# Group 0 of a hypergraph block: c2 by one product with ones, half of W2 scaled by ScalarE, squares ahead of the readings

## The chip, the core and the metric

The kernel runs on one core of one Trainium2 chip. The metric is the device time of one execution in microseconds (us). The engines are TensorE (PE; its weight loads are PEld), VectorE (DVE), ScalarE (ACT), GpSimd (POOL) and SyncE (SP), which only issues transfers here. Each runs its own list of instructions in the order written; semaphores tie the lists together.

## What is computed

For each of 64 graphs (128 nodes, 256 features) a hypergraph convolution to 512 features, ReLU, a layer norm with gamma and beta, a second convolution back to 256 features, two additions of x, and a last layer norm:

```
H = (adj != 0);  w = adj[:, 0, :]
conv(x, W, b) = Dn * H @ (Be * H^T @ (x @ W^T)) + b      Dn = 1 / (H @ w),  Be = 1 / H.sum(axis=1)
h = relu(conv(x, W1, b1))
h = layer_norm(h) * gamma + beta
out = layer_norm(x + conv(h, W2, b2) + x)
```

The norm over the 512 hidden features is folded into the second weight. W2 is turned, scaled by gamma and centred. What beta contributes, the vector c2 = W2 @ beta (256 numbers), is the same for all nodes and is added when the second layer's product is read.

## The kernel before

The 64 graphs are worked on in G = 16 groups of four. For one group the steps are: h = (adj != 0) on VectorE (make_h, L665); its transpose, for the first three groups on TensorE (turn_h, L245), then by DMA (L182); its reading with row counts by ScalarE (read_ht, L487); inverse counts (make_b, L688) and scaling (make_htb, L501); the product s (make_s, L255), degrees (make_d, L674), the scaled matrix a (L510), its transpose (L266, L518); u = x times that (make_u, L272); four products v with W1 (make_v, L285), each followed by a relu (L544) on ScalarE; the four r chunks are split into a high part on GpSimd (L985) and a low part on VectorE (L726); the products with W2 (make_g, L307), one for each graph; the second norm's statistics; y (make_y, L333); z; the last norm; the store.

The variance of a node comes from the squares of r: ScalarE squares the four chunks (square, L551), VectorE adds them in two pairs and then the pairs (add_squares, L744: three additions, the last gives q_sb), TensorE turns q into bank 3 of bank_g (turn_q, L325), and ScalarE sums it (sum_q, L565). make_g(i, 3) writes the same bank 3 afterwards, and waits for those sums.

Products in high and low parts are written as three terms. Plain fp32 products take two records each in the trace.

W2 is made ready during the first layer of group 0. TensorE turns it into banks 2 and 3 of bank_g, VectorE scales the four chunks by gamma into w2_g (scale_w2, L781) and adds them (L867, L870); one product with ones gives the sums over all hidden features (sum_w2, L387), VectorE centres by them (centre_w2, L789); ScalarE rounds to w2_hi (L615), VectorE takes the rest, w2_lo (split_w2, L796). make_g(0, 0) waits for w2_lo.

For c2, ScalarE copies the turned W2 into w2_t (L610), GpSimd writes beta along 128 columns (L1021), and TensorE makes four products, two before make_s(1) and two after (make_c2, L392); VectorE copies the result (read_c2, L801) ahead of make_h(3).

The order is written out by hand for each engine. On TensorE group 0 is lines L415 to L468, on ScalarE L604 to L661, on VectorE L861 to L925. A number in brackets after a step is the group, and after it the chunk or graph: make_v(0, 2) is chunk 2 of group 0.

Of the kernel before, what the change touches and what calls it, by code (L numbers as in the profile page):

```python
# [20 lines left out]
def hypergraph_block(nc, x, adj, W1, b1, gamma, beta, W2, b2, out):  # L21
# [13 lines left out]
    with ExitStack() as ctx:  # L35
        def sb(name, shape, dt=F32):
            return ctx.enter_context(nc.sbuf_tensor(name, shape, dt))

        def sem(name):
            return ctx.enter_context(nc.semaphore(name))  # L40
# [11 lines left out]
        vec = sb("vec", [P, 3 * KH])  # L52
        w1_hi = sb("w1_hi", [P, KD, HID], F32R)
        w1_lo = sb("w1_lo", [P, KD, HID], F32R)
        w2_t = sb("w2_t", [P, KH, DOUT])
        w2_g = sb("w2_g", [P, KH, DOUT])
        w2_sum = sb("w2_sum", [P, KH // 2, DOUT])
        beta_b = sb("beta_b", [P, KH, P])
        w2_hi = sb("w2_hi", [P, KH, W2COLS], F32R)
        w2_lo = sb("w2_lo", [P, KH, DOUT], F32R)  # L60
        c2 = sb("c2", [P, DOUT])
# [66 lines left out]
        consts_zeroed, consts_ready = sem("consts_zeroed"), sem("consts_ready")  # L128
        vec_turned, vec_ready = sem("vec_turned"), sem("vec_ready")
        w1_turned, w1_hi_ready, w1_ready = sem("w1_turned"), sem("w1_hi_ready"), sem("w1_ready")  # L130
        w2_turned, w2_t_ready, w2_scaled = sem("w2_turned"), sem("w2_t_ready"), sem("w2_scaled")
        w2_added, w2_summed, w2_centred = sem("w2_added"), sem("w2_summed"), sem("w2_centred")
        w2_hi_ready, w2_ready = sem("w2_hi_ready"), sem("w2_ready")
        beta_ready, c2_made, c2_ready = sem("beta_ready"), sem("c2_made"), sem("c2_ready")
        h_ready, h_turned, ht_ready = sem("h_ready"), sem("h_turned"), sem("ht_ready")
        h_dma_turned = sem("h_dma_turned")
        d_stored, d_row_in = sem("d_stored"), [sem("d_row_even"), sem("d_row_odd")]
# [106 lines left out]
        def _(pe):  # L244
            def turn_h(j):  # L245
                pe.wait_ge(h_ready, j + 1)
                if j == 1:
                    pe.wait_ge(at_ready, 1)
                elif j == 2:
                    pe.wait_ge(a_ready, 2)  # L250
                for n in range(PER):
                    mm = pe.transpose(bank_h_bf[:, graph(n)], h_sb[:, j % 2, n], ident_b[:, :])
                mm.then_inc(h_turned, 1)
# [18 lines left out]
            def make_u(j):  # L272
                pe.wait_ge(at_ready, j + 1)
                pe.wait_ge(x_in[j % 3], landed(j, 3))
                for c in range(KD):
                    if j == 1:
                        pe.wait_ge(relu_ready, 3 + c)
                    else:
                        pe.wait_ge(z_ready, 2 * j - 3 + c)
                    for n in range(PER):  # L280
                        mm = pe.matmul(bank_v[:, c, graph(n)], x_sb[:, j % 3, n, graph(c)], at_sb[:, j % 3, n],  # L281
                                       start=True, stop=True)
                    mm.then_inc(u_made, 1)
# [41 lines left out]
            def turn_q(i):  # L325
                pe.wait_ge(q_ready, i + 1)
                pe.wait_ge(q_summed, i * 2)
                pe.wait_ge(g_ready, i * 2)
                for n in range(PER):
                    mm = pe.transpose(turned_q[:, graph(n)], q_sb[:, graph(n)], ident[:, :])  # L330
                mm.then_inc(q_turned, 1)
# [57 lines left out]
                pe.matmul(bank_g[:, 0, 0:DOUT], ones[:, :], w2_sum[:, 0], start=True,  # L389
                          stop=True).then_inc(w2_summed, 1)  # L390

            def make_c2(chunks):  # L392
                pe.wait_ge(beta_ready, 1)
                pe.wait_ge(w2_t_ready, 1)
                for k in chunks:
                    mm = pe.matmul(bank_g[:, 1, 0:DOUT], beta_b[:, k], w2_t[:, k], start=(k == 0), stop=(k == KH - 1))
                if chunks[-1] == KH - 1:
                    mm.then_inc(c2_made, 1)

            pe.wait_ge(consts_ready, 2)  # L400
            for _ in range(WARM_UP):
# [21 lines left out]
            make_v(0, 2)  # L423
            sum_w2()
            make_v(0, 3)
            make_c2([0, 1])
            make_s(1)
            make_c2([2, 3])

            pe.wait_ge(w2_ready, 1)  # L430
            for i in range(G):
                make_g(i, 0)
                if i == 0:
                    turn_a(1)
                    turn_h(2)
                    pe.wait_ge(c2_ready, 1)
                make_g(i, 1)
                if i == 0:
                    make_u(1)
                if i == LAST:  # L440
                    turn_q(i)
                elif i:
                    make_v(i + 1, 0)
                make_g(i, 2)
                if i == 0:
                    turn_q(0)
                    make_v(1, 0)
                    make_s(2)
                elif i < LAST:
                    make_v(i + 1, 1)  # L450
                make_g(i, 3)
                if i == LAST:
                    break
                if i == 0:
                    make_v(1, 1)
                make_v(i + 1, 2)
                make_v(i + 1, 3)
                if i == 0:
# [27 lines left out]
        def _(act):  # L486
# [23 lines left out]
            def make_a(j):  # L510
                act.wait_ge(d_ready, j + 1)
                act.wait_ge(a_turned, j)
                for n in range(PER):
                    ins = nc.scalar.activation(a_sb[:, n], s_parts[:, n // 2, n % 2, 0:P], ACT.Copy,
                                               scale=dinv[:, j % 2, n:n + 1])
                ins.then_inc(a_ready, 1)

            def read_at(j):  # L518
                act.wait_ge(a_turned, j + 1)
                nc.scalar.activation(at_sb[:, j % 3].rearrange("p n c -> p (n c)"), turned_a,  # L520
                                     ACT.Copy).then_inc(at_ready, 1)
# [22 lines left out]
            def relu(i, k):  # L544
                act.wait_ge(v_made, i * KH + (k + 1))
                if i:
                    act.wait_ge(r_lo_ready, (i - 1) * KH + (k + 1))
                nc.scalar.activation(r_sb[:, k], bank_v[:, k % 2], ACT.Relu,  # L548
                                     bias=vec[:, k:k + 1]).then_inc(relu_ready, 1)
# [45 lines left out]
            for n in each(0):  # L595
# [7 lines left out]
            split_w1(1)  # L603
            split_u(0)  # L604
            act.wait_ge(vec_ready, 1)
            relu(0, 0)
            read_ht(1)
            relu(0, 1)
            act.wait_ge(w2_scaled, 2)
            nc.scalar.activation(w2_t[:, :, :].rearrange("p k o -> p (k o)"),  # L610
                                 bank_g[:, 2:4].rearrange("p b o -> p (b o)"), ACT.Copy).then_inc(w2_t_ready, 1)
            relu(0, 2)
            make_htb(1)
            act.wait_ge(w2_centred, 1)
            nc.scalar.activation(w2_hi[:, :, 0:DOUT], w2_g[:, :, :], ACT.Copy).then_inc(w2_hi_ready, 1)  # L615
            relu(0, 3)
            make_a(1)
            read_at(1)
            read_ht(2)
            square(0, 0)  # L620
            square(0, 1)
            square(0, 2)
            square(0, 3)

            for i in range(G):
                if i == 0:
# [37 lines left out]
        def _(dve):  # L664
# [113 lines left out]
                nc.vector.tensor_scalar(var2[:, last, part], mv_sb[:, last, part, 1], EPS, None,  # L778
                                        ALU.add).then_inc(var2_ready, 1)

            def scale_w2(chunks):  # L781
                dve.wait_ge(w2_turned, 1 + chunks[0] // (KH // 2))
                dve.wait_ge(vec_ready, 1)
                for k in chunks:
                    ins = nc.vector.tensor_scalar(w2_g[:, k], bank_g[:, 2 + k // 2, (k % 2) * DOUT:(k % 2 + 1) * DOUT],
                                                  vec[:, KH + k:KH + k + 1], None, ALU.mult)
                ins.then_inc(w2_scaled, 1)
# [8 lines left out]
            def split_w2():  # L796
                dve.wait_ge(w2_hi_ready, 1)
                nc.vector.tensor_tensor(w2_lo[:, :, :], w2_g[:, :, :], w2_hi[:, :, 0:DOUT].bitcast(F32),  # L798
                                        ALU.subtract).then_inc(w2_ready, 1)

            def read_c2():  # L801
                dve.wait_ge(c2_made, 1)
                nc.vector.tensor_copy(c2[:, :], bank_g[:, 1, 0:DOUT]).then_inc(c2_ready, 1)

            def make_first_h(half):
                dve.wait_ge(adj_in[0] if half else first_adj, 16)
# [54 lines left out]
            make_h(1)  # L861
            split_w1(1)
            split_u(0)
            scale_w2(range(KH // 2))
            scale_w2(range(KH // 2, KH))
            dve.wait_ge(w2_scaled, 2)
            nc.vector.tensor_tensor(w2_sum[:, :, :], w2_g[:, 0:2], w2_g[:, 2:4], ALU.add).then_inc(w2_added, 1)  # L867
            make_b(1)
            dve.wait_ge(w2_added, 1)
# [1 line left out]
            split_r(0, 0)  # L871
            centre_w2()
            split_r(0, 1)
            make_h(2)
            split_w2()
            make_d(1)
            split_r(0, 2)
            split_r(0, 3)
            read_c2()
            make_h(3)  # L880
            make_b(2)

            for i in range(LAST):
                if i == 0:
# [69 lines left out]
        def _(pool):  # L954
# [63 lines left out]
            copy_w(1)  # L1018
            pool.wait_ge(consts_ready, 3)
            pool.wait_ge(vec_ready, 1)  # L1020
            for k in range(KH):  # L1021
                ins = nc.gpsimd.tensor_scalar(beta_b[:, k], ones[:, :], vec[:, 2 * KH + k:2 * KH + k + 1], 1.0,
                                              ALU.mult, ALU.mult)
            ins.then_inc(beta_ready, 1)
            pool.wait_ge(weights_in[3], 16)
            nc.gpsimd.tensor_scalar(b2_half[:, :], b2_half[:, :], 0.5, 1.0, ALU.mult,
                                    ALU.mult).then_inc(consts_ready, 1)
# [47 lines left out]
```

## Time and profile before

| what | value |
|---|---|
| median of 3 runs | 287.64 us (287.48 to 287.89) |
| the profiled execution, its time | 287.23 us |
| its span, first to last instruction | 285.4 us |
| share of TensorE in the chain that ended last | 91% |
| TensorE busy | 276.9 us (97%) |
| VectorE busy | 229.5 us (80%) |
| ScalarE busy | 196.2 us (69%) |
| GpSimd busy | 134.9 us (47%) |
| mean granted clock of TensorE | 0.995 |

How to read it: the engines overlap, so the busy times don't add up to the span. A view in order of time gives for each instruction (or merged run of like ones) its start, its length, the line of the kernel, what it writes and from what, and in brackets how long the engine had stood idle before it and which instruction released it. Matmuls are pipelined, so a record lasts longer than the step to the next one: where a cost on TensorE is meant, take the difference of two starts. On VectorE and ScalarE too the next instruction can start up to some 0.1 us before the one before it ends.

### The profile page before, as it was taken

The page shows a single profiled execution, that of the slowest core. Times are in us where ns is not written, and L with a number is a line of the kernel's source. Part 1 is how long each engine was busy: PE and PEld are TensorE (multiplying, and loading weights), DVE is VectorE, ACT ScalarE, POOL GpSimd, SP SyncE. Part 2 cuts the span into 40 slices and gives each one's busy share as a digit, 9 for nine tenths or more (in the row PEclk, how much of TensorE's full clock was granted, in tenths as well). Part 3 has the DMA queues.
Part 4 walks back from the last instruction along what each step waited for, and adds up shares of the span by engine and source line. Part 5 has one row for each costly group of instructions (what it writes and reads, how often), then busy time and mean ns, then how long its engine had stood idle before and what let it go on. Part 6 is the DMA issues. An engine that isn't in the chain of part 4 may idle for free.

```text
span 285.4 us, 5786 instructions
## 1 busy us (share of the span) xinstructions
PE 276.9 (97%) x1820; PEld 247.8 (87%) x1820; DVE 229.5 (80%) x646; ACT 196.2 (69%) x560; POOL 134.9 (47%) x194
## 2 busy tenths in 40 slices
PE   7999999999999999999999999999999999999991
PEld 6889899898988989898998989899898989889890
DVE  3795688887889878887978878797987879696784
ACT  3588967877767678766767776676678775573714
POOL 2341546436372744536363553636364364526362
PEclk9999999999999999999999999999999999999998
DMA  6912042344324134433433333522423332020014
GB/s 217 332 52 69 3 129 39 92 126 116 114 63 158 57 97 128 111 113 92 147 54 119 112 92 112 111 94 55 149 39 92 94 93 76 37 73 3 21 54 147
DMA packets 37270, 27.70 MB, mean 97 GB/s; under 512 B 10028, under 2 KB 35320, under 8 KB 37240
## 3 DMA queue, kind: packets, MB, share of 16 engines
q1 hardware_dynamic: 37136, 27.30, 33.8%
q8 instruction: 14, 0.23, 0.3%
q14 instruction: 16, 0.13, 0.2%
q10 hardware_dynamic: 104, 0.04, 0.1%
HBM read 17.21 MB, written 8.42 MB: 90 GB/s over the span
## 4 chain that ended last, share of the span: by engine, by line
PE 91%; ACT 3%; DVE 3%; issue 1%; POOL 1%; DVEq 0%; POOLq 0%; ACTq 0%
PE bank_v L303 30%; PE bank_g L320 10%; PE bank_v L337 10%; PE bank_g L313 10%; PE bank_g L315 10%; PE bank_v L281 8%; PE bank_s L262 4%; PE bank_g L330 3%; PE bank_s L402 1%; ACT ht_sb L497 1%; ACT sq_sb L555 1%; PE bank_g L383 1%; DVE bn_sb L933 1%; DVE q_sb L742 0%; DVE pair_sb L735 0%
## 5 line engine op out<-in xcount | busy, mean ns | idle before, releaser
L981 POOL TENSOR_TENSOR xb_sb<-x_sb,b_half 128x512 f32<-128x512 f32 (+1 forms) x31 | 41.1, 1329 | 76.0 <-DVE r_lo L730 51.1
L548 ACT ACTIVATE r_sb<-bank_v,vec 128x512 f32<-128x512 f32 x64 | 44.2, 690 | 38.0 <-PE bank_v L303 37.4
L313 PE MATMUL bank_g<-w_hi,r_hi 128*128 128x258 f32 x256 | 65.6, 288 | 0.0
L315 PE MATMUL bank_g<-w_lo,r_hi 128*128 128x256 f32 x256 | 63.8, 282 | 0.0
L989 POOL TENSOR_SCALAR r_hi<-r_sb 128x512 fp32r<-128x512 f32 x64 | 43.6, 682 | 39.8 <-ACT r_sb L548 39.8
L303 PE MATMUL bank_v<-u_hi,w_lo 128*128 128x512 f32 x128 | 50.8, 397 | 0.0
L303 PE MATMUL bank_v<-u_lo,w_hi 128*128 128x512 f32 x128 | 50.8, 397 | 0.0
L303 PE MATMUL bank_v<-u_hi,w_hi 128*128 128x512 f32 x128 | 50.7, 396 | 0.0
L313 PEld LDWEIGHTS bank_g<-w_hi,r_hi 128*128 128x128 f32 x256 | 48.3, 189 | 1.7 <-DVE w_lo L798 0.3
L730 DVE TENSOR_TENSOR r_lo<-r_sb,r_hi 128x512 fp32r<-128x512 f32 x64 | 48.9, 785 | 0.9 <-POOL r_hi L989 0.9
L315 PEld LDWEIGHTS bank_g<-w_lo,r_hi 128*128 128x128 f32 x256 | 48.1, 188 | 1.2
L320 PE MATMUL bank_g<-w_hi,r_lo 128*128 128x258 f32 x256 | 41.5, 283 | 0.1
L555 ACT ACTIVATE sq_sb<-r_sb 128x512 f32<-128x512 f32 x64 | 40.2, 634 | 1.9
L721 DVE SCALAR_TENSOR_TENSOR g_sb<-bank_g,rstd,c 128x256 f32<-128x256 f32 x64 | 28.1, 480 | 12.8 <-POOL rstd L965 12.8
L320 PEld LDWEIGHTS bank_g<-w_hi,r_lo 128*128 128x128 f32 x256 | 35.3, 189 | 0.3 <-DVE r_lo L730 0.3
L560 ACT ACTIVATE z_sb<-z_sb,shift,rstd 128x256 f32<-128x256 f32 x60 | 32.3, 586 | 4.5 <-POOL shift L1004 4.5
L526 ACT ACTIVATE u_hi<-bank_v 128x512 fp32r<-128x512 f32 x30 | 17.9, 600 | 24.3 <-PE bank_v L281 24.3
L337 PE MATMUL bank_v<-g_sb,at_sb 128*128 128x256 f32 x120 | 31.7, 387 | 0.1
L965 POOL TENSOR_TENSOR rstd<-stat,half_power 128x2 f32<-128x2 f32 x32 | 22.6, 708 | 18.3 <-DVE stat L711 18.1
L281 PE MATMUL bank_v<-at_sb,x_sb 128*128 128x128 f32 x240 | 29.4, 276 | 0.0
L303 PEld LDWEIGHTS bank_v<-u_lo,w_hi 128*128 128x128 f32 x128 | 24.0, 188 | 6.1 <-DVE u_lo L698 0.7
L337 PEld LDWEIGHTS bank_v<-g_sb,at_sb 128*128 128x128 f32 x120 | 21.5, 189 | 8.2 <-issue 5.3
(119 smaller groups left out, 457.6 us busy)
## 6 DMA issues: line engine op xcount, KB each, us to landing
x_sb<-in_x_dram SPq DMA_DIRECT2D x16, 512.0 KB, 3.9
out_dram<-z_sb SPq DMA_DIRECT2D x15, 512.0 KB, 3.2
adj_sb<-in_adj_dram SPq DMA_DIRECT2D x15, 256.0 KB, 3.7
d_row<-d_rows SPq DMA_DIRECT2D x13, 256.0 KB, 3.7
w_raw<-in_L_gnn_W_dram SPq DMA_DIRECT2D x2, 512.0 KB, 4.9
out_dram<-z_sb SPq DMA_DIRECT2D x2, 256.0 KB, 2.4
adj_sb<-in_adj_dram SPq DMA_DIRECT2D x2, 128.0 KB, 2.4
turned_h<-h_sb SPq DMA_TRANSPOSE x13, 2.4
```

Of the source, the lines that this page charges most:

```text
L281: mm = pe.matmul(bank_v[:, c, graph(n)], x_sb[:, j % 3, n, graph(c)], at_sb[:, j % 3, n], start=True, stop=True)
L303: mm = pe.matmul(bank_v[:, k % 2], w[:, c, graph(k)], u[:, c], start=(m == 0), stop=(m == len(terms) - 1))
L313: pe.matmul(bank_g[:, n, 0:W2COLS], r_hi[:, i % 2, k, graph(n)], w2_hi[:, k], start=(k == 0), stop=False)
L315: pe.matmul(bank_g[:, n, 0:DOUT], r_hi[:, i % 2, k, graph(n)], w2_lo[:, k], start=False, stop=False, skip_group_check=True)
L320: mm = pe.matmul(bank_g[:, n, 0:W2COLS], r_lo[:, i % 2, k, graph(n)], w2_hi[:, k], start=False, stop=(k == KH - 1))
L337: mm = pe.matmul(bank_v[:, half, (n % 2) * DOUT:(n % 2 + 1) * DOUT], at_sb[:, i % 3, n], g_sb[:, n], start=True, stop=True)
L548: nc.scalar.activation(r_sb[:, k], bank_v[:, k % 2], ACT.Relu, bias=vec[:, k:k + 1]).then_inc(relu_ready, 1)
L555: nc.scalar.activation(sq_sb[:, k], r_sb[:, k], ACT.Square).then_inc(sq_ready, 1)
L560: ins = nc.scalar.activation(z_sb[:, i % 2, n], z_sb[:, i % 2, n], ACT.Identity, bias=shift2[:, n:n + 1], scale=rstd2[:, 0, n:n + 1])
L730: nc.vector.tensor_tensor(r_lo[:, i % 2, k], r_sb[:, k], r_hi[:, i % 2, k].bitcast(F32), ALU.subtract).then_inc(r_lo_ready, 1)
L981: nc.gpsimd.tensor_tensor(xb_sb[:, i % 2, part], x_sb[:, i % 3, part], b2_half[:, :].unsqueeze(1).to_broadcast([P, n, DOUT]), ALU.add).the ...
L989: nc.gpsimd.tensor_scalar(r_hi[:, i % 2, k], r_sb[:, k], 1.0, 1.0, ALU.mult, ALU.mult).then_inc(r_hi_ready, 1)
```

## The change

The four c2 products are replaced by one. VectorE forms, in four instructions, the sum over the chunks of turned W2 times beta, straight from banks 2 and 3, and TensorE multiplies it once by ones, into bank 3. This product stands behind make_u(1) and ahead of make_g(0, 2); turn_q(0), which writes the same bank, waits for the copy of c2. The copies w2_t and beta_b are gone. ScalarE scales chunks 0 and 1 of W2 by gamma ahead of relu(0, 0), and VectorE only chunks 2 and 3. turn_h(2) goes behind make_g(0, 1); make_h(2) behind the last r_lo of group 0; read_c2 behind make_b(2). ScalarE squares chunk 0 ahead of make_a(1), chunk 1 ahead of read_at(1), and reads ht(2) last.

```diff
 TensorE
-            def make_c2(chunks):
-                pe.wait_ge(beta_ready, 1)
-                pe.wait_ge(w2_t_ready, 1)
-                for k in chunks:
-                    mm = pe.matmul(bank_g[:, 1, 0:DOUT], beta_b[:, k], w2_t[:, k], start=(k == 0), stop=(k == KH - 1))
...
+            def make_c2():
+                pe.wait_ge(beta_added, KH)
+                pe.matmul(bank_g[:, 3, 0:DOUT], ones[:, :], w2_beta[:, (KH - 1) % 2], start=True,
+                          stop=True).then_inc(c2_made, 1)
...
             make_v(0, 3)
-            make_c2([0, 1])
             make_s(1)
-            make_c2([2, 3])
...
                 if i == 0:
                     turn_a(1)
-                    turn_h(2)
-                    pe.wait_ge(c2_ready, 1)
                 make_g(i, 1)
                 if i == 0:
+                    turn_h(2)
                     make_u(1)
+                    make_c2()
...
                 make_g(i, 2)
                 if i == 0:
+                    pe.wait_ge(c2_ready, 1)
                     turn_q(0)
 ScalarE
             act.wait_ge(vec_ready, 1)
+            act.wait_ge(w2_turned, 1)
+            for k in range(KH // 2):
+                ins = nc.scalar.activation(w2_g[:, k], bank_g[:, 2, k * DOUT:(k + 1) * DOUT], ACT.Copy,
+                                           scale=vec[:, KH + k:KH + k + 1])
+            ins.then_inc(w2_low_scaled, 1)
             relu(0, 0)
...
-            act.wait_ge(w2_scaled, 2)
-            nc.scalar.activation(w2_t[:, :, :].rearrange("p k o -> p (k o)"),
-                                 bank_g[:, 2:4].rearrange("p b o -> p (b o)"), ACT.Copy).then_inc(w2_t_ready, 1)
...
             relu(0, 3)
+            square(0, 0)
             make_a(1)
+            square(0, 1)
             read_at(1)
-            read_ht(2)
-            square(0, 0)
-            square(0, 1)
             square(0, 2)
             square(0, 3)
+            read_ht(2)
 VectorE
+            def add_beta(k):
+                w2_t, scale = bank_g[:, 2 + k // 2, (k % 2) * DOUT:(k % 2 + 1) * DOUT], vec[:, 2 * KH + k:2 * KH + k + 1]
+                if k == 0:
+                    ins = nc.vector.tensor_scalar(w2_beta[:, 0], w2_t, scale, None, ALU.mult)
+                else:
+                    dve.wait_ge(beta_added, k)
+                    ins = nc.vector.scalar_tensor_tensor(out=w2_beta[:, k % 2], in0=w2_t, scalar=scale,
+                                                         in1=w2_beta[:, (k - 1) % 2], op0=ALU.mult, op1=ALU.add)
+                ins.then_inc(beta_added, 1)
...
             split_r(0, 1)
-            make_h(2)
             split_w2()
             make_d(1)
             split_r(0, 2)
             split_r(0, 3)
-            read_c2()
+            make_h(2)
+            for k in range(KH):
+                add_beta(k)
             make_h(3)
             make_b(2)
+            read_c2()
 
             for i in range(LAST):
                 if i == 0:
                     add_squares(0)
 GpSimd
-            for k in range(KH):
-                ins = nc.gpsimd.tensor_scalar(beta_b[:, k], ones[:, :], vec[:, 2 * KH + k:2 * KH + k + 1], 1.0,
-                                              ALU.mult, ALU.mult)
-            ins.then_inc(beta_ready, 1)
```

## Rows read from the trace of the kernel before

**Rows 1.** Waits of TensorE: engine, line, releaser: us in total, times, longest.

```profile
PE bank_s L402 <- POOL ident L1011: 1.8, 1, 1.8
PE bank_g L330 <- DVE q_sb L742: 0.3, 1, 0.3
```

**Rows 2.** Timeline of TensorE: start, us, line, what [idle before <- releaser].

```profile
16.54 0.59 PE L389 MATMUL bank_g<-w_sum,ones 128*128 128x256 f32 x2
...
18.37 1.03 PE L396 MATMUL bank_g<-w_t,beta_b 128*128 128x256 f32 x4
19.24 1.05 PE L262 MATMUL bank_s<-htb_sb,ht_sb 128*128 128x129 f32 x8
20.13 1.03 PE L396 MATMUL bank_g<-w_t,beta_b 128*128 128x256 f32 x4
21.06 0.39 PE L313 MATMUL bank_g<-w_hi,r_hi 128*128 128x258 f32 x1
...
25.12 1.95 PE L281 MATMUL bank_v<-at_sb,x_sb 128*128 128x128 f32 x16
26.82 0.37 PE L313 MATMUL bank_g<-w_hi,r_hi 128*128 128x258 f32 x1
...
28.82 0.66 PE L330 MATMUL bank_g<-ident,q_sb 128*128 128x128 f32 x4 [0.32 <-DVE q_sb L742]
29.42 0.50 PE L303 MATMUL bank_v<-u_hi,w_hi 128*128 128x512 f32 x1
```

**Rows 3.** Timeline of the weight loads, the first of make_g(0, 0).

```profile
21.06 0.19 PEld L313 LDWEIGHTS bank_g<-w_hi,r_hi 128*128 128x128 f32 x1 [0.31 <-DVE w_lo L798]
```

**Rows 4.** Timeline of VectorE.

```profile
17.25 1.40 DVE L792 SCALAR_TENSOR_TENSOR w_g<-bank_g,w_g 128x256 f32<-128x256 f32 x4
...
19.78 1.23 DVE L798 TENSOR_TENSOR w_lo<-w_g,w_hi 128x1024 fp32r<-128x1024 f32 x1 [0.19 <-ACT w_hi L615]
...
21.41 1.28 DVE L730 TENSOR_TENSOR r_lo<-r_sb,r_hi 128x512 fp32r<-128x512 f32 x2
22.61 0.42 DVE L803 COPY c<-bank_g 128x256 f32<-128x256 f32 x1
22.94 0.42 DVE L671 TENSOR_SCALAR h_sb<-adj_sb 128x512 bf16<-128x512 f32 x1
...
26.31 0.69 DVE L735 TENSOR_TENSOR pair_sb<-sq_sb 128x512 f32<-128x512 f32 x1 [0.65 <-ACT sq_sb L555]
27.35 0.69 DVE L735 TENSOR_TENSOR pair_sb<-sq_sb 128x512 f32<-128x512 f32 x1 [0.35 <-ACT sq_sb L555]
28.07 0.69 DVE L742 TENSOR_TENSOR q_sb<-pair_sb 128x512 f32<-128x512 f32 x1
28.68 1.28 DVE L698 TENSOR_TENSOR u_lo<-bank_v,u_hi 128x512 fp32r<-128x512 f32 x2
```

**Rows 5.** Timeline of ScalarE.

```profile
13.71 0.69 ACT L548 ACTIVATE r_sb<-bank_v,vec 128x512 f32<-128x512 f32 x1 [1.38 <-PE bank_v L303]
...
18.69 1.06 ACT L615 ACTIVATE w_hi<-w_g 128x1024 fp32r<-128x1024 f32 x1
...
24.10 0.27 ACT L497 ACTIVATE ht_sb<-bank_s 128x128 f32<-128x128 bf16 x1
...
25.10 2.21 ACT L555 ACTIVATE sq_sb<-r_sb 128x512 f32<-128x512 f32 x4
...
30.48 0.28 ACT L570 ACTIVATE scratch<-bank_g 128x128 f32<-128x128 f32 x1
```

**Rows 6.** Groups of VectorE by form, the reading of g: busy us, mean ns.

```profile
L721 DVE SCALAR_TENSOR_TENSOR g_sb<-bank_g,rstd,c 128x256 f32<-128x256 f32 x64 | 28.1, 480 | 12.8 <-POOL rstd L965 12.8
```

**Rows 7.** The page, part 6: the DMA transposes of h, us from issue to landing.

```profile
turned_h<-h_sb SPq DMA_TRANSPOSE x13, 2.4
```

**Rows 8.** Stretches of 1 us in the tail: busy of PE, PEld, DVE, ACT, POOL, granted clock.

```profile
281.00:282.00 1.00, 0.00 (x0) 0.00 (x0) 0.36 (x1) 0.64 (x2) 0.54 (x1) 1.00 0.57 205
...
283.00:284.00 1.00, 0.00 (x0) 0.00 (x0) 0.00 (x0) 0.00 (x0) 0.00 (x0) 0.50 1.00 343
```

More of the change, by code:

```diff
@@ L54, in hypergraph_block @@
         w1_lo = sb("w1_lo", [P, KD, HID], F32R)
-        w2_t = sb("w2_t", [P, KH, DOUT])
+        w2_beta = sb("w2_beta", [P, 2, DOUT])
         w2_g = sb("w2_g", [P, KH, DOUT])
         w2_sum = sb("w2_sum", [P, KH // 2, DOUT])
-        beta_b = sb("beta_b", [P, KH, P])
         w2_hi = sb("w2_hi", [P, KH, W2COLS], F32R)
@@ L130, in hypergraph_block @@
         w1_turned, w1_hi_ready, w1_ready = sem("w1_turned"), sem("w1_hi_ready"), sem("w1_ready")
-        w2_turned, w2_t_ready, w2_scaled = sem("w2_turned"), sem("w2_t_ready"), sem("w2_scaled")
+        w2_turned, w2_low_scaled, w2_scaled = sem("w2_turned"), sem("w2_low_scaled"), sem("w2_scaled")
         w2_added, w2_summed, w2_centred = sem("w2_added"), sem("w2_summed"), sem("w2_centred")
         w2_hi_ready, w2_ready = sem("w2_hi_ready"), sem("w2_ready")
-        beta_ready, c2_made, c2_ready = sem("beta_ready"), sem("c2_made"), sem("c2_ready")
+        beta_added, c2_made, c2_ready = sem("beta_added"), sem("c2_made"), sem("c2_ready")
         h_ready, h_turned, ht_ready = sem("h_ready"), sem("h_turned"), sem("ht_ready")
@@ L390, in sum_w2 @@
                           stop=True).then_inc(w2_summed, 1)
-            def make_c2(chunks):
-                pe.wait_ge(beta_ready, 1)
-                pe.wait_ge(w2_t_ready, 1)
-                for k in chunks:
-                    mm = pe.matmul(bank_g[:, 1, 0:DOUT], beta_b[:, k], w2_t[:, k], start=(k == 0), stop=(k == KH - 1))
-                if chunks[-1] == KH - 1:
-                    mm.then_inc(c2_made, 1)
+            def make_c2():
+                pe.wait_ge(beta_added, KH)
+                pe.matmul(bank_g[:, 3, 0:DOUT], ones[:, :], w2_beta[:, (KH - 1) % 2], start=True,
+                          stop=True).then_inc(c2_made, 1)
             pe.wait_ge(consts_ready, 2)
@@ L779, in make_var2, with scale_w2 @@
                                         ALU.add).then_inc(var2_ready, 1)
-            def scale_w2(chunks):
-                dve.wait_ge(w2_turned, 1 + chunks[0] // (KH // 2))
+            def scale_w2():
+                dve.wait_ge(w2_turned, 2)
                 dve.wait_ge(vec_ready, 1)
-                for k in chunks:
+                for k in range(KH // 2, KH):
                     ins = nc.vector.tensor_scalar(w2_g[:, k], bank_g[:, 2 + k // 2, (k % 2) * DOUT:(k % 2 + 1) * DOUT],
@@ L799, in split_w2 @@
                                         ALU.subtract).then_inc(w2_ready, 1)
+            def add_beta(k):
[7 more added lines that the diff above has]
+                ins.then_inc(beta_added, 1)
             def read_c2():
                 dve.wait_ge(c2_made, 1)
-                nc.vector.tensor_copy(c2[:, :], bank_g[:, 1, 0:DOUT]).then_inc(c2_ready, 1)
+                nc.vector.tensor_copy(c2[:, :], bank_g[:, 3, 0:DOUT]).then_inc(c2_ready, 1)
             def make_first_h(half):
@@ L863, in _ @@
             split_u(0)
-            scale_w2(range(KH // 2))
-            scale_w2(range(KH // 2, KH))
-            dve.wait_ge(w2_scaled, 2)
+            scale_w2()
+            dve.wait_ge(w2_scaled, 1)
+            dve.wait_ge(w2_low_scaled, 1)
             nc.vector.tensor_tensor(w2_sum[:, :, :], w2_g[:, 0:2], w2_g[:, 2:4], ALU.add).then_inc(w2_added, 1)
```

## The prediction, made before the changed kernel was run

> **What bounds the kernel now.** I read the waits of TensorE first: over the whole run its matmul stream stopped for another engine twice, 1.8 us at the very start and 0.3 us before the turning of q [rows 1]. So every us by which TensorE's stream is stretched or halted is a us on the end, and nothing later can absorb it, because no later idle of TensorE exists to shrink. (The page's chain of work says the same: nearly all of it lies on TensorE.) All that the change touches lies in group 0, between 12 and 30 us. There I read the start times on TensorE [rows 2], its weight loads, which show what the next product was held by [rows 3], and the two engines that feed it [rows 4, 5].
>
> What the reader is to see in these: make_g(0, 0) starts at 21.06, and its weight load had waited 0.31 us for w2_lo, which ends at 19.78 + 1.23 = 21.01 [rows 3, 4]. The second half of the c2 products, at 20.13, occupies TensorE only up to that moment [rows 2]: it fills a wait. The next stop is q: VectorE finishes q_sb at 28.07 + 0.69 = 28.76, the transposes start at 28.82, 0.06 later [rows 2, 4]. The one after is the low half of u: u_lo's first chunk ends at 28.68 + 0.69 = 29.37 and make_v(1, 0) starts at 29.42 [rows 2, 4]. From there TensorE runs without a stop [rows 1].
>
> **The change, part by part.** The sum is made for the start of turn_q(0) and of make_v(1, 0), 28.82 and 29.42 before; what they shift by, the end shifts by.
>
> (a) Eight c2 records leave TensorE ahead of make_g(0, 0): 0.87 us at 18.37 to 19.24 and some 0.87 us from 20.13 [rows 2]. They gain nothing by themselves, because w2_lo decides the start. make_s(1) can follow, though not before htb(1), which is ready when ScalarE goes to w2_hi, at 18.69 [rows 5]; it takes 0.89 us (19.24 to 20.13), so TensorE then stands idle from about 19.55 to 21.0, 1.4 us.
>
> (b) How much sooner w2_lo can be. ScalarE loses the copy w2_t, as long as w2_hi's pass over the same 1024 columns, 1.06 us [rows 5]. But w2_hi, at 18.69, also needs VectorE's centring, 17.25 + 1.40 = 18.65, and that needs the sum product, two records from 16.54 to 17.13, which can start no sooner since it stands behind make_v(0, 2) [rows 2, 4]. So of the whole copy at most 0.1 us arrives at w2_lo. I take 0.05 us (bounds 0 and 0.1).
>
> (c) Scaling half of W2 on ScalarE: two instructions of 256 columns. The trace has none of that form; a pass over 1024 columns takes 1.06 us, one relu over 512 takes 0.69, so each lies between a quarter of the first and the whole of the second: 0.5 to 1.4 us for both. They fall into a wait of 1.38 us ahead of relu(0, 0) at 13.71 [rows 5]. Cost nothing. VectorE is freed of two scalings, but what it made with them, the sum of W2, is wanted by a product that stands behind make_v(0, 2) on TensorE and was on hand when it got there: no wait of TensorE lies there [rows 1]. Gain nothing. The four beta broadcasts taken from GpSimd ran ahead of its first splitting of r: nothing either way.
>
> (d) After w2_lo VectorE keeps its order, d(1) and the last two r_lo (21.41 + 1.28 = 22.69), which make_g(0, 0) needs for its last product [rows 4]. So make_u(1) starts at 25.12 - 0.05 = 25.07: turn_h(2) merely changes places with make_g(0, 1) (0.20 us either side), and the transposes of a are as before.
>
> (e) VectorE's new sum. It starts after make_h(2), about 22.9. Four instructions of 128x256 from PSUM with a scalar by partition: the nearest row is the reading of g, 0.48 us [rows 6], and each waits for the one before, so 4 x 0.51 = 2.0 us, done by 24.9; make_h(3), 0.42, by 25.3. The bound below is the centring, 1.40 us for four with no waits [rows 4]; above I allow 0.6 us each, 2.4 us. TensorE asks for the sum at 26.77: cover of 1 us or more by either bound. Cost nothing. make_h(2) comes 3.3 us later and make_h(3) 1.9 us later; on SP's queue the load of adj(5) waits for the one, the DMA transpose of h(3) for the other, and the load of adj(6) behind it. The transposes take 2.4 us from issue to landing in the median [rows 7]; from 25.3 that is 27.7, and ScalarE comes to read ht(3) only near 28.8. Adj(5) isn't read before group 1. Nothing; the price of a transpose 2 us longer than that would be 1 us on ScalarE ahead of sum_q(0), which (g) shows to have a us to spare.
>
> (f) The new c2 product: one fp32 product of 256 columns with ones, two records. Four such take 0.87 us [rows 2], so 0.44 us. It stands behind make_u(1), at 26.82 - 0.05 = 26.77. The result is complete 0.59 us after its start (as the sum product's), at 27.36, and VectorE sees it 0.05 us later: 27.41.
>
> (g) The step that decides. read_c2 stands on VectorE ahead of add_squares(0). In the kernel before it ran at 22.61, when c2 was long there, and add_squares could start at 26.31 as soon as ScalarE had two squares; the last square ended at 25.10 + 2.21 = 27.31 [rows 4, 5]. Now ScalarE squares before the reading of at(1) and ht(2) and ends near 25.3, 2 us sooner, but VectorE cannot use it: it has finished make_b(2) at about 26.8 (turn_h(2) ends at 25.1, ScalarE's four readings, 1.0 us from 24.10 to 25.10 [rows 5], and two small instructions follow) and waits for c2 until 27.41. What is queued behind that wait is the chain for q. The copy of c2 costs 0.42 us, of which 0.33 before the next starts (22.61 to 22.94): 27.74. First pair 0.61, second pair 0.69 + 0.03, q 0.69, in all 2.02 us (by the two r_lo of 1.28 us, and from 27.35 to 28.07) [rows 4]: q at 29.76. turn_q(0) at 29.82 instead of 28.82: **1.00 us later**. split_u(1) follows q on VectorE as before, so make_v(1, 0) starts 1.00 us later too. make_g(0, 2) ends, with the 0.44 us of c2 in front of it, at about 28.7, so TensorE idles 1.1 us there instead of 0.3. ScalarE's sum_q(0) came at 30.48 only since ScalarE was busy till then [rows 5]; with q turned at 30.5 it hardly moves, and make_g(0, 3), at 32.7, doesn't wait for it.
>
> Sum: -0.05 (w2_lo) + 1.05 (q) = +1.00 us, carried to the end. The profiled execution has a span of 285.4 us and took 287.23; the median of the runs is 287.64, 0.4 above. On the profiled execution I expect a span of 286.4 and a time of 288.2; on the median, 288.6 us. For the likeliest case alone the unknown terms are the sooner w2_lo (0 to 0.1), the c2 product with its latency (0.5 to 0.8) and the copy (0.33 to 0.5), so +0.8 to +1.3 and 288.4 to 288.9.
>
> **The clock.** TensorE's granted clock is 1.00 (2.4 GHz) in every stretch up to the tail; at the end TensorE does nothing after 279.3, and the clock is still 1.00 in 281 to 282 and is 0.50 in 283 to 284 [rows 8]. So it outlasted over 2.7 us without work; the two new idle stretches, 1.4 and 1.1 us with 8 us of products between, are shorter. I count no loss. The Trainium skill, page "TensorE: Matmul & The Clock Gate", Part 1, says that an engine which has been idle is set back to 1.2 GHz and must be busy for a time to get 2.4 GHz back; by it the idle that this change opens could cost a slow stretch, and that speaks against the change. As a mechanism here: if one of the stops brought the clock to 0.50, as it stands after 283 [rows 8], a slow stretch as long as the one seen there (some 2.8 us to the end of the span) would do half its work, 1.4 us more.
>
> **Rivals.**
> Squares sooner makes q sooner (the other side). If VectorE were not held, the adds could run from 26.8 and q would not hold TensorE: turn_q(0) directly behind make_g(0, 2), which now ends near 28.7, and make_v(1, 0) at 29.15 to 29.3, 0.1 to 0.3 sooner: 287.4. For it: the squares really are 2 us sooner, and the wait for them was the last to end. It decides if c2 is on hand when VectorE gets to read_c2, so if make_u(1) ended by 26.2, 0.6 us earlier than it can by (d). Little speaks for it: 0.10.
> Part of the loss comes back, so that +0.2 to +0.55 is left: the copy of c2 and the pair adds cost less than I took, or TensorE had hidden slack in group 1. Against it, TensorE starts its products there at their steady spacing: 0.10; about 288.0.
> The chain ahead of w2_lo shrinks by the whole copy (1.06 us) and c2 is hidden: 286.6. Against it stands the centring, as in (b): 0.04.
> The clock falls in one of the stops: 1.00 + 1.4 = 2.4 us, 290.0: 0.05.
> The forecast has 0.71.
>
> **How the numbers follow.** About 0.2% (0.58 us) is what a measurement of this kernel can tell from no change. Slower by more than that: forecast and clock, 0.76. Within it: the first two rivals, 0.20. Faster: 0.04. The range, 287.6 to 289.1, takes in the forecast's own bounds with 0.2 us of spread between runs and the partly returned loss; it leaves out most of the quicker cases and the clock, about 2 in 10.
>
> **What would show it.** In the trace of the changed kernel: an idle stretch of TensorE of 1.4 us ending at 21.0, with w2_lo as its releaser; c2's product at 26.8; VectorE idle before the copy of c2 with that product as releaser; the copy at 27.4, the first pair add right behind it though the squares had been done since about 25.3; TensorE idle for 1.1 us before the transposes of q, now at 29.8; then start times of group 1 one us later than before to the end. I am wrong if c2's product comes well ahead of 26, if VectorE doesn't wait at the copy, if the granted clock drops below 1.00 near 20 or 30 us, or if TensorE closes the gap later on.

## The result, and the profile after

The changed kernel took 288.39 us (median of 11 runs, 288.13 to 288.82) against 287.48 us (287.17 to 287.89, 11 runs) for the kernel before beside it: ratio 1.0033, 95% interval 1.0024 to 1.0043. The profiled execution took 288.13 us, with a span of 286.3 us, 0.9 more than before. The forecast was 1.0 us slower.

TensorE's waits after (engine, line, releaser: us in total, times, longest), to be read beside [rows 1]:

```profile
PE bank_s L398 <- POOL ident L1021: 1.8, 1, 1.8
PE bank_g L312 <- DVE w_lo L795: 1.2, 1, 1.2
PE bank_g L329 <- issue: 1.1, 1, 1.1
```

The 0.3 us ahead of the transposes of q has become 1.1 us, and 1.2 us of idle has opened ahead of make_g(0, 0). "issue" in the third line says that no releaser was recognised; the VectorE rows below show which one it was. The fourth line of that view, 0.6 us for L365, lies in the first 6 us and has no part in this.

TensorE in order of time after (start, us, line, what, idle before), beside [rows 2]:

```profile
18.64 1.16 PE L261 MATMUL bank_s<-htb_sb,ht_sb 128*128 128x129 f32 x8
20.98 0.39 PE L312 MATMUL bank_g<-w_hi,r_hi 128*128 128x258 f32 x1 [1.19 <-DVE w_lo L795]
...
25.00 2.00 PE L280 MATMUL bank_v<-at_sb,x_sb 128*128 128x128 f32 x16
26.84 0.60 PE L393 MATMUL bank_g<-w_beta,ones 128*128 128x256 f32 x2
27.09 0.47 PE L312 MATMUL bank_g<-w_hi,r_hi 128*128 128x258 f32 x1
...
29.93 0.63 PE L329 MATMUL bank_g<-ident,q_sb 128*128 128x128 f32 x4 [1.06 <-issue]
30.48 0.50 PE L302 MATMUL bank_v<-u_hi,w_hi 128*128 128x512 f32 x1
```

VectorE after, beside [rows 4]:

```profile
19.70 1.23 DVE L795 TENSOR_TENSOR w_lo<-w_g,w_hi 128x1024 fp32r<-128x1024 f32 x1 [0.53 <-ACT w_hi L612]
...
22.53 0.42 DVE L668 TENSOR_SCALAR h_sb<-adj_sb 128x512 bf16<-128x512 f32 x1
22.86 0.47 DVE L802 TENSOR_SCALAR w_beta<-bank_g,vec 128x256 f32<-128x256 f32 x1
23.37 1.52 DVE L805 SCALAR_TENSOR_TENSOR w_beta<-bank_g,vec,w_beta 128x256 f32<-128x256 f32 x3
24.81 0.42 DVE L668 TENSOR_SCALAR h_sb<-adj_sb 128x512 bf16<-128x512 f32 x1
26.38 0.17 DVE L687 TENSOR_SCALAR binv<-members 128x4 f32<-128x4 f32 x1 [1.15 <-ACT ht_sb L492]
26.58 0.18 DVE L690 RECIPROCAL binv<-binv 128x4 f32<-128x4 f32 x1
27.48 0.42 DVE L811 COPY c<-bank_g 128x256 f32<-128x256 f32 x1 [0.72 <-PE bank_g L393]
27.82 1.28 DVE L732 TENSOR_TENSOR pair_sb<-sq_sb 128x512 f32<-128x512 f32 x2
29.14 0.69 DVE L739 TENSOR_TENSOR q_sb<-pair_sb 128x512 f32<-128x512 f32 x1
```

ScalarE after, beside [rows 5]:

```profile
12.22 0.83 ACT L603 ACTIVATE w_g<-bank_g,vec 128x256 f32<-128x256 f32 x2
13.64 0.69 ACT L543 ACTIVATE r_sb<-bank_v,vec 128x512 f32<-128x512 f32 x1 [0.59 <-PE bank_v L302]
...
18.61 1.06 ACT L612 ACTIVATE w_hi<-w_g 128x1024 fp32r<-128x1024 f32 x1
...
24.02 1.14 ACT L550 ACTIVATE sq_sb<-r_sb 128x512 f32<-128x512 f32 x2
...
30.60 0.28 ACT L565 ACTIVATE scratch<-bank_g 128x128 f32<-128x128 f32 x1 [0.62 <-PE bank_g L329]
```

Read them together. The squares end at 24.02 + 1.14 = 25.16. VectorE does nothing from 25.2 to 26.38, then two small instructions, then nothing for 0.72 us until c2 is made (26.84 + 0.60 = 27.44). Only behind the copy, at 27.82, does it begin to add squares that have lain ready for 2.7 us. It finishes q at 29.83; the transposes start at 29.93.

**A measure that is steadier than the span.** The start of make_g(0, 0) differed between the profiled executions of this study, 20.98 to 21.79. It follows what comes before it: the first transposes of W1 began at 6.69 in the executions before and after and at 7.16 in e7 below. What put them off I didn't follow up. All that the change and the experiments touch behind w2_lo lies between the start of make_g(0, 0) and the start of make_v(1, 0). From the second turning of q on, all ten profiled executions took the same time to the start of the last product on the banks of s: 235.71 to 235.76 us. So I cut each timeline at three starts (all in us):

| kernel | make_g(0, 0) | to turn_q(0) | to make_v(1, 0) | from there to turn_q(1) | ratio to before, 95% interval |
|---|---|---|---|---|---|
| before | 21.06 | 7.76 | 8.36 | 12.95 | |
| changed | 20.98 | 8.95 | 9.50 | 12.87 | 1.0033 (1.0024 to 1.0043) |
| e1, c2 ahead of u | 21.58 | 8.13 | 8.68 | 12.87 | 1.0014 (1.0005 to 1.0022) |
| e2, copy behind the pairs | 21.38 | 8.00 | 8.55 | 12.87 | 1.0000 (0.9991 to 1.0009) |
| e3, squares late | 21.54 | 8.99 | 9.54 | 12.94 | 1.0048 (1.0035 to 1.0060) |
| e4, squares only, in before | 21.38 | 7.60 | 8.20 | 12.86 | 0.9995 (0.9986 to 1.0004) |
| e5, changed again | 21.05 | 8.94 | 9.50 | 12.86 | 1.0045 (1.0029 to 1.0061) |
| e6, c2 late in before | 21.22 | 9.36 | 9.92 | 12.86 | 1.0061 (1.0040 to 1.0082) |
| e7, squares and adds | 21.79 | 7.31 | 7.66 | 13.08 | 0.9983 (0.9974 to 0.9992) |
| e8, c2 in the gap | 21.08 | 7.31 | 7.66 | 13.06 | 0.9984 (0.9972 to 0.9996) |

For the changed kernel: 9.50 - 8.36 = +1.14, start -0.08, group 1 -0.08, and the rest of the stream -0.05; the last product starts at 279.06 against 278.13, +0.93, which is the 0.9 us of the span and of the medians.

### The profile page after: what moved, and what is told of

Read it like the earlier page. It is cut to its first block, busy times and chain, and to the rows that moved or that the text cites. A ratio compares the mean times of both kernels' runs of the same rounds, so it can differ in the third digit from the quotient of the medians.

```text
span 286.3 us, 5772 instructions
## 1 busy us (share of the span) xinstructions
PE 275.2 (96%) x1814; PEld 246.1 (86%) x1814; DVE 229.8 (80%) x648; ACT 196.8 (69%) x561; POOL 134.0 (47%) x190
## 4 chain that ended last, share of the span: by engine, by line
PE 93%; DVE 3%; issue 1%; ACT 1%; POOL 1%; DVEq 0%; POOLq 0%
PE bank_v L302 31%; PE bank_g L319 11%; PE bank_g L312 11%; PE bank_g L314 10%; PE bank_v L336 10%; PE bank_v L280 9%; PE bank_s L261 4%; PE bank_g L329 3%; PE bank_s L398 1%; PE bank_g L382 1%; DVE bn_sb L943 1%; DVE w_g L789 0%; DVE w_lo L795 0%; PE bank_s L365 0%; ACT w_hi L612 0%
## 5 line engine op out<-in xcount | busy, mean ns | idle before, releaser
L999 POOL TENSOR_SCALAR r_hi<-r_sb 128x512 fp32r<-128x512 f32 x64 | 44.3, 692 | 38.8 <-ACT r_sb L543 38.8
```

What stands on the lines that cost most here:

```text
L999: nc.gpsimd.tensor_scalar(r_hi[:, i % 2, k], r_sb[:, k], 1.0, 1.0, ALU.mult, ALU.mult).then_inc(r_hi_ready, 1)
```

## The experiments

The theory: VectorE's copy of c2 stands ahead of the adds of the squares, c2 is made only behind make_u(1), and so q and with it TensorE wait. The rival: the cost is TensorE's own, the c2 product where nothing hides it. A second rival: it depends on how soon the squares come.

**e1, c2 sooner on TensorE.**

```diff
-                    make_u(1)
-                    make_c2()
+                    make_c2()
+                    make_u(1)
```

> The changed kernel with one move on TensorE: the c2 product ahead of make_u(1) instead of behind it. Same work on every engine. Theory (VectorE's wait for c2, ahead of the adds of the squares, holds q): c2 is made by 25.6, VectorE copies it right behind make_b(2) with no wait, at 26.7, the adds start at 27.0 and not 27.8, turn_q(0) starts at 29.1 and not 29.93, make_v(1, 0) at 29.7 and not 30.48: 0.8 us faster than the changed kernel, about 0.1% slower than the kernel before. Rival (the 0.44 us of the c2 product in TensorE's stream behind the hidden place, plus the idle ahead of make_g(0, 0), is the cost): nothing changes, 0.3% slower than the kernel before.

Measured: 287.79 us, 1.0014 (1.0005 to 1.0022). From make_g(0, 0) to make_v(1, 0) 8.68 us, 0.82 less than in the changed kernel, where 0.8 was expected. VectorE in e1:

```profile
27.19 0.18 DVE L690 RECIPROCAL binv<-binv 128x4 f32<-128x4 f32 x1
27.29 0.39 DVE L811 COPY c<-bank_g 128x256 f32<-128x256 f32 x1
27.60 1.28 DVE L732 TENSOR_TENSOR pair_sb<-sq_sb 128x512 f32<-128x512 f32 x2
```

The copy follows make_b(2) with no wait, and the adds 0.31 us later. TensorE's work is the same to the product, only its order differs. The first rival falls; by it nothing would have changed.

**e2, the copy behind the pair adds.**

```diff
             make_b(2)
-            read_c2()
...
                 if i == 0:
-                    add_squares(0)
+                    add_pair(0, 0)
+                    add_pair(0, 1)
+                    read_c2()
+                    add_pairs(0)
```

> The changed kernel with one move on VectorE: the copy of c2 between the two pair adds and the last add of group 0, instead of ahead of all three. TensorE's order is untouched. Theory: the pair adds start at 26.7, the copy follows at 27.9 without a wait, q is done at 28.9, turn_q(0) starts at 29.0, make_v(1, 0) at 29.6: 0.9 us faster than the changed kernel, 0 to 0.1% slower than the kernel before. Rival (cost lies in TensorE's stream): no change against the changed kernel, 0.3% slower than the kernel before.

Measured: 287.29 us, 1.0000 (0.9991 to 1.0009): the loss is gone. 8.55 us to make_v(1, 0), 0.95 less than in the changed kernel. VectorE in e2:

```profile
27.08 1.26 DVE L732 TENSOR_TENSOR pair_sb<-sq_sb 128x512 f32<-128x512 f32 x2
28.26 0.42 DVE L811 COPY c<-bank_g 128x256 f32<-128x256 f32 x1
28.59 0.68 DVE L739 TENSOR_TENSOR q_sb<-pair_sb 128x512 f32<-128x512 f32 x1
```

and TensorE, the end of make_g(0, 2) and the transposes of q:

```profile
28.64 0.64 PE L319 MATMUL bank_g<-w_hi,r_lo 128*128 128x258 f32 x4
29.38 0.63 PE L329 MATMUL bank_g<-ident,q_sb 128*128 128x128 f32 x4
```

The c2 product stands where it stood, in TensorE's stream behind make_u(1), and the copy is as long as before. Only what was queued behind the wait has changed. It was not the product, nor the copy's length, but the wait ahead of the adds.

Differences of starts show how much of the loss is TensorE's own. From the start of make_g(0, 0) to the last four products of make_g(0, 2) it takes 7.26 us here and 7.25 in the changed kernel, against 6.80 before: the product costs 0.45 us of its stream. From those four products to the transposes of q it takes 0.49 us in e7 and e8 below, where q is early, 0.96 in the kernel before, 1.70 in the changed kernel and 0.74 here. So TensorE waited 0.47 us for q before the change, which is room for the product, and waits 1.21 us after it. In e2 it still waits 0.25 us, although no idle is listed, because a matmul record is longer than the step to the next one; q, done at 29.27, is what sets the remaining 0.19 us against the kernel before.

**e3, the squares in their old order, in the changed kernel.**

```diff
             relu(0, 3)
-            square(0, 0)
             make_a(1)
-            square(0, 1)
             read_at(1)
+            read_ht(2)
+            square(0, 0)
+            square(0, 1)
             square(0, 2)
             square(0, 3)
-            read_ht(2)
```

> The changed kernel with ScalarE's old order: the four squares of group 0 behind the readings of at(1) and ht(2). Theory: the squares end at 28.3 instead of 25.2, but VectorE gets to its adds only at 27.8 and needs the last two squares at 28.4, so q and turn_q(0) move by 0 to 0.1 us; sum_q(0) ends near 32.8, just as make_g(0, 3) asks for it: the same as the changed kernel within 0.2 us. Rival (how soon the squares are there decides q): q follows the last square by 1.4 us plus some queueing and comes 1 to 3 us later, 0.4 to 1% slower than the changed kernel.

Measured: 288.84 us, 1.0048 (1.0035 to 1.0060). The squares end at 26.77 + 2.20 = 28.97, 7.4 us after make_g(0, 0) starts, against 4.2 us in the changed kernel, and make_v(1, 0) comes 9.54 us after it instead of 9.50. VectorE in e3:

```profile
28.03 0.42 DVE L811 COPY c<-bank_g 128x256 f32<-128x256 f32 x1 [0.72 <-PE bank_g L393]
28.37 1.33 DVE L732 TENSOR_TENSOR pair_sb<-sq_sb 128x512 f32<-128x512 f32 x2
29.73 0.69 DVE L739 TENSOR_TENSOR q_sb<-pair_sb 128x512 f32<-128x512 f32 x1
```

Three us on the squares moved q by 0.04 us. Behind the wait for c2 the new order is worth almost nothing. The trace bears out "the same within 0.2 us" (0.04, and 0.07 in group 1); the ratio, with an interval that overlaps those of both measurements of the changed kernel, can't tell a tenth.

**e4, the squares' order alone, in the kernel before.** The edit is the reverse of e3's, made to the kernel before.

> The kernel before with the one part 'squares of group 0 sooner': ScalarE squares chunk 0 ahead of make_a(1), chunk 1 ahead of read_at(1), chunks 2 and 3 ahead of read_ht(2). Nothing else. Theory (VectorE's list in order decides q): make_b(2), ahead of the adds, now waits for the later reading of ht(2), to 26.7; the adds end at 28.7 against 28.76, turn_q(0) starts at most 0.1 us sooner: the same as the kernel before within 0.1%. Rival (the squares were the bound and their coming sooner by 2 us frees q): turn_q(0) directly behind make_g(0, 2), make_v(1, 0) 0.3 to 0.5 us sooner, 0.1 to 0.2% faster.

Measured: 287.10 us, 0.9995 (0.9986 to 1.0004): the same. By the trace turn_q(0) comes 0.16 us sooner (7.60 for 7.76), a little more than the 0.1 expected and far from the 2 us by which the squares came sooner. VectorE in e4:

```profile
23.26 0.42 DVE L671 TENSOR_SCALAR h_sb<-adj_sb 128x512 bf16<-128x512 f32 x1
26.63 0.17 DVE L690 TENSOR_SCALAR binv<-members 128x4 f32<-128x4 f32 x1 [2.95 <-ACT ht_sb L497]
26.84 0.18 DVE L693 RECIPROCAL binv<-binv 128x4 f32<-128x4 f32 x1
26.93 1.26 DVE L735 TENSOR_TENSOR pair_sb<-sq_sb 128x512 f32<-128x512 f32 x2
```

Here c2 is early and no wait for it exists, and still VectorE stands for 2.95 us with squares at hand, because make_b(2) is next in its list and waits for ht(2), whose reading the new order has put behind the squares. What ScalarE gives sooner, VectorE's order takes back for the most part. The second rival falls in both kernels.

**e5, the changed kernel again**, beside e6 to e8.

> The changed kernel itself, beside the three that follow: 0.3% slower than the kernel before. From the start of make_g(0, 0) to the start of make_v(1, 0) 9.5 us, against 8.36 in the kernel before.

Measured: 288.67 us, 1.0045 (1.0029 to 1.0061), and 9.50 us to make_v(1, 0) once more. The ratio is a tenth of a per cent above the first one, with an interval that overlaps its; the trace gives the same times to 0.01 us.

**e6, the cause alone, in the kernel before.** The products go into bank 3, the last two behind make_u(1), and the copy ahead of the adds.

```diff
             make_s(1)
-            make_c2([2, 3])
...
                     make_u(1)
+                    make_c2([2, 3])
...
+                    pe.wait_ge(c2_ready, 1)
                     turn_q(0)
...
             split_r(0, 3)
-            read_c2()
             make_h(3)
             make_b(2)
+            read_c2()
```

> The kernel before with the suspected cause alone: its four c2 products (into bank 3), the last two of them moved behind make_u(1), and the copy of c2 moved behind make_b(2), ahead of the adds of the squares; turn_q(0) waits for the copy. ScalarE's order, the copy w2_t and the scaling of W2 stay as they were. Theory (c2 late, and its copy ahead of the adds): the two products take 0.87 us behind make_u(1), c2 is complete about 7.0 us after make_g(0, 0) starts, VectorE waits for it with the squares at hand or nearly so, q follows 2.4 us later, and make_g(0, 0) to make_v(1, 0) takes 9.8 to 9.9 us instead of 8.36: 0.45 to 0.5% slower than the kernel before. Rival (the loss comes from the other parts, squares and scaling): only TensorE's own 0.87 us less the wait of 0.3 us it had there, 0.2% slower.

Measured: 288.82 us, 1.0061 (1.0040 to 1.0082); 9.92 us to make_v(1, 0), where 9.8 to 9.9 was expected. TensorE in e6, the two late products:

```profile
27.06 1.03 PE L396 MATMUL bank_g<-w_t,beta_b 128*128 128x256 f32 x4
```

and VectorE behind them:

```profile
28.13 0.42 DVE L803 COPY c<-bank_g 128x256 f32<-128x256 f32 x1 [2.32 <-PE bank_g L396]
28.47 1.28 DVE L735 TENSOR_TENSOR pair_sb<-sq_sb 128x512 f32<-128x512 f32 x2
29.79 0.69 DVE L742 TENSOR_TENSOR q_sb<-pair_sb 128x512 f32<-128x512 f32 x1
```

Squares in the old order, scaling as before, w2_t copied as before, and the loss is there, larger by what the second product adds (1.56 us to make_v(1, 0) for 1.14, 0.42 more). The rival, TensorE's own cost alone, would have made it 0.2%. From the end of c2 to the turning of q: 30.58 - 28.09 = 2.49 us here, 29.93 - 27.44 = 2.49 us in the changed kernel. The chain is the same one.

**e7, the squares sooner and the adds where they can use it**, in the kernel before with e4's order.

```diff
             make_h(3)
+            add_squares(0)
             make_b(2)
 
             for i in range(LAST):
-                if i == 0:
-                    add_squares(0)
```

> The kernel before with the squares of group 0 sooner on ScalarE, as in the change, and the three adds of the squares on VectorE ahead of make_b(2), whose wait held them. Nothing else. Theory (VectorE's list in order decides q, the squares alone are worth nothing): q is done 5.5 us after make_g(0, 0) starts and turn_q(0) stands directly behind make_g(0, 2); split_u(1) too comes sooner; make_g(0, 0) to make_v(1, 0) takes 7.8 to 7.9 us instead of 8.36: 0.15 to 0.2% faster than the kernel before. Rival (another wait takes its place: htb(2), the reading of ht(3) and sum_q(0) on ScalarE hold make_g(0, 3)): the gain is given back there, no change.

Measured: 287.01 us, 0.9983 (0.9974 to 0.9992), faster than both kernels. VectorE in e7:

```profile
24.00 0.68 DVE L735 TENSOR_TENSOR pair_sb<-sq_sb 128x512 f32<-128x512 f32 x1
26.01 0.69 DVE L735 TENSOR_TENSOR pair_sb<-sq_sb 128x512 f32<-128x512 f32 x1 [1.32 <-ACT sq_sb L555]
26.73 0.69 DVE L742 TENSOR_TENSOR q_sb<-pair_sb 128x512 f32<-128x512 f32 x1
```

q is done 5.6 us after make_g(0, 0) starts, ahead of any need, and its transposes stand directly behind make_g(0, 2). 7.66 us to make_v(1, 0), 0.70 less than before (I expected 0.5); 0.13 us of it is lost again up to turn_q(1) (13.08 against 12.95), of which make_g(0, 3), now 2.40 us behind make_v(1, 0) and not 2.31, has 0.09. What is left, 0.57 us, agrees with the 0.49 us of the ratio. The rival held a small part.

**e8, c2 in the idle stretch ahead of make_g(0, 0)**, in the changed kernel, with the adds as in e7.

```diff
 TensorE
             make_s(1)
+            make_c2()
...
                     make_u(1)
-                    make_c2()
 VectorE, behind the first sum of W2
+            add_beta(0)
+            add_beta(1)
             make_b(1)
...
             split_r(0, 0)
+            add_beta(2)
             centre_w2()
             split_r(0, 1)
+            add_beta(3)
             split_w2()
...
             make_h(2)
-            for k in range(KH):
-                add_beta(k)
+            read_c2()
             make_h(3)
+            add_squares(0)
             make_b(2)
-            read_c2()
```

> The changed kernel with c2 made in the idle stretch that the change opens on TensorE ahead of make_g(0, 0): VectorE sums W2 times beta in its own waits there (two steps behind the first sum of W2, one ahead of the centring, one ahead of w2_lo), the product stands behind make_s(1), the copy ahead of make_h(3), and the adds of the squares ahead of make_b(2). Theory: the product costs TensorE nothing, q is early, make_g(0, 0) to make_v(1, 0) takes 7.9 to 8.1 us; the extra steps on VectorE may put off the centring and so w2_lo by 0 to 0.4 us; 0.0 to 0.15% faster than the kernel before. Rival (one product by the sum is dearer for VectorE than four on TensorE wherever it stands): slower than the kernel before.

Measured: 286.95 us, 0.9984 (0.9972 to 0.9996). VectorE in e8:

```profile
16.79 0.48 DVE L805 SCALAR_TENSOR_TENSOR w_beta<-bank_g,vec,w_beta 128x256 f32<-128x256 f32 x1
17.26 1.42 DVE L789 SCALAR_TENSOR_TENSOR w_g<-bank_g,w_g 128x256 f32<-128x256 f32 x4
...
19.80 1.22 DVE L795 TENSOR_TENSOR w_lo<-w_g,w_hi 128x1024 fp32r<-128x1024 f32 x1
```

and TensorE:

```profile
18.73 1.16 PE L261 MATMUL bank_s<-htb_sb,ht_sb 128*128 128x129 f32 x8
19.73 0.70 PE L393 MATMUL bank_g<-w_beta,ones 128*128 128x256 f32 x2
```

The centring starts at 17.26 against 17.16 in the changed kernel and w2_lo at 19.80 against 19.70, but make_s(1) too starts 0.09 us later in this execution (18.73 against 18.64): the four steps put off w2_lo by nothing that shows. The product runs in TensorE's idle time. One product for four is neither dearer nor cheaper than the old way: e7 and e8 take the same 7.66 us, and can't be told apart by time. What the change's form of c2 is worth depends on where it stands.

## Why the prediction was right

Point by point, by its steps:

- (a) The idle ahead of make_g(0, 0) is there: 1.19 us, and 1.4 was said. The last record of make_s(1) ends at 18.64 + 1.16 = 19.80; the prediction counted the idle from the step to a next start, 0.2 us sooner.
- (b) w2_lo sooner by 0.05, bound 0.1: it started at 19.70 against 19.78, 0.08 sooner, and w2_hi at 18.61 against 18.69. The centring, at 17.16, started when the sum product was done (16.53 + 0.59 = 17.12), which is the bound that the prediction named. Before the change it started at 17.25 [rows 4], 0.12 after that product was done: r_lo(0, 0) held it there (last section), which the prediction did not see.
- (c) Two scalings on ScalarE, 0.5 to 1.4 us in a wait of 1.38: 0.83 us, with 0.59 us of the wait left. VectorE's shorter share bought nothing at the product: sum_w2 started at 16.53 against 16.54. "Gain nothing" was not quite so behind it: VectorE came to r_lo(0, 0) 0.22 us sooner, at 16.01 for 16.23, and that is what let the centring start sooner. The scaling was not run by itself; this rests on the two traces.
- (d) make_u(1) at 25.07: 25.00. The rest of the early path was as said.
- (e) The sum over the chunks in 2.0 us: 22.86 to 24.89, 2.03 us. 1.95 us of cover were left when TensorE asked for it at 26.84. The turned h(3) was in time: ScalarE read it at 28.71 without a wait.
- (f) The product at 26.77, c2 complete for VectorE at 27.41: 26.84 and 27.48. The 0.07 is in make_u(1), which with turn_h(2) ahead of it and c2's product behind it took 1.84 us to the next start where the prediction kept the old 1.70 (1.76 in e8, with turn_h(2) ahead of it alone).
- (g) VectorE waits for c2: 0.72 us (0.6 by the prediction's times 26.8 and 27.41). From c2 to the turning of q 2.41 us were expected and 2.45 measured (27.48 to 29.93). The 0.04 lies between the end of q and the transposes: 0.10 us, and 0.10 to 0.11 in all the other runs with the wait for c2_ready in front of turn_q and q the last to come, against 0.06 in the kernel before and in e4. turn_q(0) at 29.82: 29.93. make_v(1, 0) 1.00 later: 1.06. sum_q(0) hardly moved, 30.60 against 30.48 [rows 5], as said.
- Carried to the end: 0.13 us were not. From turn_q(1) on the two executions take the same time to 0.05 us, but between make_v(1, 0) and turn_q(1) the changed kernel takes 12.87 us against 12.95. "Nothing later can absorb it" was too strong by a tenth. The difference lies in the products of make_u(2): 1.79 us from their start to the turning of q against 1.86. Why stays open; e1, e2, e4, e5 and e6 have the shorter time too, e3 doesn't, and e7 and e8, with an early q, pay 0.1 us more in group 1.

So +1.00 was forecast, +0.93 found in TensorE's last product, and +0.91 in the medians. The mechanism is the forecast's; that the sums agree this closely is in part luck, since make_v(1, 0) came 0.06 later than said and 0.13 came back that was not said to, and since the second measurement of the same kernel (e5) put the medians 1.28 us apart.

The rivals. "Squares sooner makes q sooner" needed c2 at hand; e4 shows that it would not have come even then, since make_b(2) also stood in front, and e7 shows what it is worth with both out of the way: 0.5 us. "Part of the loss comes back" needed 0.45 us or more; 0.13 came. "The chain ahead of w2_lo shrinks by the whole copy": it shrank by 0.08, see (b). The clock: in the two stretches where TensorE did least (us, busy of PE, PEld, DVE, ACT, POOL, granted clock, DMA) the changed kernel has

```profile
20.00:21.00 1.00, 0.02 (x1) 0.02 (x1) 1.00 (x2) 0.76 (x2) 0.67 (x1) 1.00 0.00 0
...
29.00:30.00 1.00, 0.07 (x1) 0.10 (x2) 0.96 (x3) 0.98 (x8) 0.02 (x1) 1.00 0.07 18
```

The granted clock stayed at 1.00, 2.4 GHz, through both, as [rows 8] had suggested for stops of this length. By the rule of the Trainium skill (page "TensorE: Matmul & The Clock Gate", Part 1) an idle engine is set back; the stops of 1.1 and 1.2 us between products did not bring that about here.

## What to carry to other kernels

When a result is moved to a later place, look at what stands behind its reader on the reader's own engine: the copy of c2 cost 0.4 us, but its wait of 0.7 us and the copy itself held back three adds on which the busiest engine was waiting. Work made ready sooner on one engine is worth next to nothing until the consumer's list is reordered to take it: the early squares gave 0.04 us in the changed kernel and 0.16 us in the kernel before, and 0.5 us once VectorE's adds stood ahead of its next wait. And take work away from the busiest engine only where it isn't already inside a wait, here 1.2 us for w2_lo.

## What the runs showed that was not expected

GpSimd's rounding of r(0, 1) and VectorE's r_lo(0, 0) meet at 16 us, and the one that starts first pays next to nothing. Before:

```profile
16.11 0.68 POOL L989 TENSOR_SCALAR r_hi<-r_sb 128x512 fp32r<-128x512 f32 x1 [0.94 <-ACT r_sb L548]
...
16.23 1.10 DVE L730 TENSOR_TENSOR r_lo<-r_sb,r_hi 128x512 fp32r<-128x512 f32 x1
```

and after:

```profile
16.01 0.69 DVE L727 TENSOR_TENSOR r_lo<-r_sb,r_hi 128x512 fp32r<-128x512 f32 x1
16.11 1.06 POOL L999 TENSOR_SCALAR r_hi<-r_sb 128x512 fp32r<-128x512 f32 x1 [1.00 <-ACT r_sb L543]
17.16 1.42 DVE L789 SCALAR_TENSOR_TENSOR w_g<-bank_g,w_g 128x256 f32<-128x256 f32 x4 [0.47 <-PE bank_g L388]
```

The same two instructions take 0.68 and 1.10 us in the one order and 1.06 and 0.69 us in the other: the one that starts 0.1 us later is some 0.4 us longer. The other eight executions show the same, by which of the two starts first. The Trainium skill, page "SBUF — State Buffer", section "SBUF: two separate sides", says that VectorE with two inputs from SBUF and a GpSimd instruction that reads SBUF share a pair of ports which the first to start holds for its whole length. The rows agree in the order, and nearly in the size: the later one ends 0.47 to 0.54 us after the earlier, somewhat less than the 0.62 us (r_hi) or 0.68 us (r_lo) that it takes undisturbed.

It matters a little here. Before, the centring followed r_lo(0, 0), which ended at 16.23 + 1.10 = 17.33, without a wait, at 17.25 [rows 4], though TensorE's sum had been done at 17.13. In the changed kernel r_lo(0, 0) is over at 16.70 and the centring waits for the sum. From the start of the sum product to the centring it takes 0.71 to 0.72 us in the kernel before, e4, e6 and e7, and 0.63 in the changed kernel, e1, e2, e3, e5 and e8; make_g(0, 0) comes 4.52 to 4.53 us behind the sum product in the first four and 4.45 to 4.46 in the others. ScalarE came to w2_hi 0.08 us sooner too, at 18.61 for 18.69, with the copy w2_t gone from its list. The 0.08 us at w2_lo needed both; neither was run alone.
